# Vector engine waits moved to the next piece of work, and an expert factor read straight from its PSUM bank

## The chip, the cores and the metric

The kernel runs on one core of one Trainium2 chip. Its time is the time of the program on the device in microseconds. Everything else is a row of one profiled execution: TensorE (PE) multiplies matrices into eight banks of 128x512 float32, VectorE (DVE) does elementwise work and reductions, ScalarE (ACT) evaluates activations and copies out of banks, GpSimd (POOL) and SyncE (SP) issue transfers. Engines run their own queues in order and meet at semaphores.

## What is computed

Eight images of 32x32x128 go through six layers, each added to its input. All is float32.

```python
x = x + deformable_conv(_gn(x))        # 9 taps, 4 gathered corners each, weighted, then one matmul
x = x + corr_ranks(_gn(x))             # corr = x3 @ x3.T / c ; sort each row of 1024; take 128 ranks
t = tokens(x)
t = t + window_attention(_ln(t))       # windows of 4, 16, 32
t = t + moe_1(_ln(t))                  # 8 experts, top 2, gelu
t = t + state_space(_ln(t))            # chunked scan
t = t + moe_2(_ln(t))                  # see below

# second layer of the ranks
x_sort = jnp.sort(corr, axis=-1)[..., ::-1]
ranks = jnp.round(jnp.linspace(1.0, m - 1, 128)).astype(jnp.int32)
return x_sort[..., ranks]

# moe_2: the gate is applied to the tokens of the second factor
h1 = jnp.einsum('nc,ehc->neh', flat, w1)
h3 = jnp.einsum('nc,ehc->neh', flat, w3)
h = jax.nn.silu(h1) * h3
y = jnp.einsum('neh,ech->nec', h, w2)
out = jnp.einsum('ne,nec->nc', gates, y)
```

## The kernel before, in words

Four streams of work are woven on every engine. **F** is the first part of an image: group norm, the convolution's indices, 72 gathers of 128 cells (GpSimd), the weighted sums and the convolution, a second group norm, and the correlation of one half. **S** is the sort, on VectorE alone, one unit per half image of 512 tokens: 4 tiles of 128 tokens in two buffers, srt_a and srt_b, 4096 values in a partition. **C** is attention, first experts and state space for a half image. **M** is the second experts for a half image. While image i is sorted, F works on image i+1, C on the second half of i-1 and the first half of i, and M on both halves of i-1. So there are a fill (F alone), an early stage (F, S, C), six full stages (F, S, C, M), a late stage (S, C, M) and a drain (C, M).

Each stream is a generator, and a piece of work ends at a `yield`. The table ORDER holds for each engine and stage a string of letters; `weave` calls the next piece of the stream that the letter names. So the order on each engine is fixed by that table, and an engine whose next piece must wait holds everything behind it.

VectorE must also wait for itself where an instruction reads what the one ahead wrote. `Chain` does this: `link(ins)` lets the instruction count up a semaphore of its stream (dve_F, dve_S, dve_C0, dve_C1, dve_M) and waits for that count at once, at the end of the piece.

The sort (`dve_S`) merges runs of 2, 4, ... 1024. A run of m is merged by a compare of its halves, and then steps of distance m/4, m/8, ... 1. Each step is a max (L813) and a min (L815) of 2048 values at most, from one buffer into the other, and a copy (L817) of the values at both edges of each run that the step leaves alone. Distances m/4 and m/8 are handled apart (L789 to L804). At the end only the 128 ranks are wanted, and three steps (L844) run in the pieces of `rank_pieces`, seven each.

The second experts (`pe_M`, `act_M`, `dve_M`) take three slices (128, 128 and 85 rows) of each of 8 experts per half image, 24 in all. For slice n TensorE multiplies w1 with the tokens into one of two banks (L1517) and w3 with the gated tokens into the other (L1521). ScalarE takes the silu of the first (L1569) into a slot of act2 and copies the second (L1575) into a slot of h3_s; each counts up m_sb, which frees the bank. VectorE multiplies the two slots (L1605, counts up hh), and TensorE uses the product three slices later (L1501). The weights of an expert come in two buffers.

## Time and profile before

| | us |
|---|---|
| runs | 5235.73, 5244.01, 5248.09; median 5244.01 |
| the profiled execution | 5253.13, its span 5251.3 |
| VectorE busy | 4484.3 (85%) |
| TensorE busy | 3963.6 (75%) |
| ScalarE busy | 3017.1 (57%) |
| a full stage, from one image's sort to the next | 601.3 |
| early stage, late stage, drain | 525.5, 567.1, 330.3 |

Busy time is the time that an engine's instructions cover, so where two overlap it is counted once. Stages are cut where the sort of an image starts on VectorE. The mean duration of an instruction is from its start to its end, and can be longer than the distance to the next start.

### The profile page before, as it was taken

Reading aid. Unit: us, or ns where it says so; the run is one execution under the profiler, and the core shown is the slowest. Engines: PE = TensorE matmul, PEld = TensorE weight load, DVE = VectorE, ACT = ScalarE, POOL = GpSimd, SP = SyncE. Lnnn points to the kernel's source line nnn. Section 1 sums busy time; section 2 is a strip of 40 time slices with the busy share of each in tenths; the row PEclk is TensorE's granted clock in tenths of the full one; section 3 lists DMA queues with packets and bytes.
Section 4 is the critical chain, followed back from the end, with each engine's and each line's share of the span. In section 5 each row is a group of like instructions: output and inputs, shape, how many; then the busy total and the mean of one; then the engine's idle time right before and its main releaser. Section 6 shows DMA issues by size and latency. Waiting matters only on the chain.

```text
span 5251.3 us, 59990 instructions
## 1 busy us (share of the span) xinstructions
PE 3963.6 (75%) x19026; PEld 2690.2 (51%) x19026; DVE 4484.3 (85%) x5651; ACT 3017.1 (57%) x7469; POOL 930.2 (18%) x580
## 2 busy tenths in 40 slices
PE   5665628887698877888688877888688877885387
PEld 4544314754366544755357543765357544553254
DVE  0297998899989998899989998999988999999621
ACT  4544326765476635875477645865467646553363
POOL 2253002600054001610045000620036000000000
PEclk8877759999898988988899988988899888886698
DMA  4232001311122011310123001310123001000001
GB/s 131 83 100 65 16 0 55 113 35 30 36 89 83 24 38 39 115 50 23 31 84 101 24 29 42 109 58 23 30 73 109 28 25 30 27 29 14 8 22 36
DMA packets 226079, 269.70 MB, mean 51 GB/s; under 512 B 26831, under 2 KB 188506, under 8 KB 225626
## 3 DMA queue, kind: packets, MB, share of 16 engines
q0 software_dynamic: 46080, 151.03, 9.6%
q1 hardware_dynamic: 179674, 114.65, 7.5%
q8 instruction: 165, 2.70, 0.2%
q14 instruction: 160, 1.31, 0.1%
HBM read 242.25 MB, written 23.34 MB: 51 GB/s over the span
## 4 chain that ended last, share of the span: by engine, by line
DVE 40%; PE 29%; issue 13%; ACT 6%; DMA 5%; SPq 4%; POOL 3%; DVEq 0%; ACTq 0%; POOLq 0%
PE bank L597 6%; DMA gath<-quads,idx 4%; DVE srt_b L772 4%; DVE srt_a L772 4%; PE bank L1204 3%; DVE srt_a L815 3%; POOL gath L735 3%; SPq L502 3%; DVE srt_b L815 3%; DVE srt_a L813 2%; DVE srt_b L804 2%; PE bank L607 2%; DVE srt_a L770 2%; DVE srt_b L813 2%; DVE act L1605 2%
## 5 line engine op out<-in xcount | busy, mean ns | idle before, releaser
L735 POOL DMA_INDIRECT gath<-quads,idx x576 | 930.0, 1615 | 3123.4 <-DVE idx L706 2585.7
L597 PE MATMUL bank<-diag,gath 128*128 128x128 f32 x4608 | 640.6, 303 | 222.3 <-DMA gath<-quads,idx 217.5
L597 PEld LDWEIGHTS bank<-diag,gath 128*128 128x128 f32 x4608 | 615.5, 217 | 269.6 <-DMA gath<-quads,idx 141.9
L630 ACT ACTIVATE diag<-ident,w 128x128 f32<-128x128 f32 x2304 | 696.3, 391 | 12.0 <-DVE w L719 12.0
L1517 PE MATMUL bank<-mu_t,e2w 128*128 128x512 f32 (+1 forms) x768 | 460.5, 685 | 198.6 <-DMA e2w<-moe_w_t 168.0
L1501 PEld LDWEIGHTS bank<-e2w,act 128*128 128x128 f32 (+1 forms) x3072 | 448.1, 214 | 212.3 <-issue 167.4
L1501 PE MATMUL bank<-e2w,act 128*128 128x128 f32 (+1 forms) x3072 | 450.8, 297 | 40.4 <-DVE act L1605 40.4
L1605 DVE TENSOR_TENSOR act<-act,h_s 128x512 f32<-128x512 f32 (+1 forms) x384 | 262.2, 686 | 243.0 <-ACT h_s L1575 231.1
L1521 PE MATMUL bank<-gated_u,e2w 128*128 128x512 f32 (+1 forms) x768 | 456.8, 680 | 15.3 <-ACT h_s L1575 11.7
L1569 ACT ACTIVATE act<-bank 128x512 f32<-128x512 f32 (+1 forms) x384 | 228.2, 594 | 347.8 <-PE bank L1517 345.8
L813 DVE TENSOR_TENSOR srt_a<-srt_b 128x1920 f32<-128x1920 f32 (+5 forms) x176 | 381.5, 2167 | 4.8 <-DVE arena L1421 0.3
L813 DVE TENSOR_TENSOR srt_b<-srt_a 128x1792 f32<-128x1792 f32 (+4 forms) x176 | 378.9, 2153 | 3.7
L815 DVE TENSOR_TENSOR srt_a<-srt_b 128x1920 f32<-128x1920 f32 (+5 forms) x176 | 380.6, 2162 | 0.2 <-DVE carry L1421 0.2
L815 DVE TENSOR_TENSOR srt_b<-srt_a 128x1792 f32<-128x1792 f32 (+4 forms) x176 | 377.9, 2147 | 0.2 <-DVE arena L1421 0.2
L770 DVE TENSOR_TENSOR srt_b<-srt_a 128x2048 f32<-128x2048 f32 x128 | 293.2, 2290 | 5.3 <-DVE srt_a L772 2.5
L772 DVE TENSOR_TENSOR srt_b<-srt_a 128x2048 f32<-128x2048 f32 x128 | 292.5, 2285 | 0.2
L1575 ACT ACTIVATE h_s<-bank 128x512 f32<-128x512 f32 (+1 forms) x384 | 227.3, 592 | 111.5 <-PE bank L1521 109.8
L663 ACT ACTIVATE cols<-bank 128x384 f32<-128x384 f32 x192 | 92.9, 484 | 318.1 <-PE bank L597 306.4
L770 DVE TENSOR_TENSOR srt_a<-srt_b 128x2048 f32<-128x2048 f32 x112 | 256.4, 2289 | 3.4 <-issue 0.5
L772 DVE TENSOR_TENSOR srt_a<-srt_b 128x2048 f32<-128x2048 f32 x112 | 255.5, 2281 | 0.0
L1517 PEld LDWEIGHTS bank<-mu_t,e2w 128*128 128x128 f32 (+1 forms) x768 | 127.6, 201 | 243.9 <-issue 128.9
L1521 PEld LDWEIGHTS bank<-gated_u,e2w 128*128 128x128 f32 (+1 forms) x768 | 144.3, 201 | 208.7 <-issue 150.6
(319 smaller groups left out, 7562.1 us busy)
## 6 DMA issues: line engine op xcount, KB each, us to landing
e2w<-moe_w_t SPq DMA_DIRECT2D x256, 170.5 KB
quads<-xn_tok SPq DMA_DIRECT2D x256, 64.0 KB
e1w<-L_ffn_w SPq DMA_DIRECT2D x256, 64.0 KB, 1.9
e2w<-moe_w_t SPq DMA_DIRECT2D x256, 64.0 KB
gath<-quads,idx POOLq DMA_INDIRECT x576
e2w<-moe_w_t SPq DMA_DIRECT2D x128, 42.5 KB
x_tok<-x SPq DMA_DIRECT2D x8, 512.0 KB, 4.0
out<-tm SPq DMA_DIRECT2D x16, 256.0 KB, 2.5
```

The source lines that it names most:

```text
L597: ins = T.matmul(FB[q % 2][:, k * P:(k + 1) * P], gath[:, g % 2, k, s * C:(s + 1) * C], diag[:, g % 2, 4 * k + s], start=(s == 0), stop=(s ...
L630: ins = SC.activation(diag[:, g % 2, n], ident[:], ACT.Copy, scale=w[:, n:n + 1])
L735: pool.indirect_dma_start(gath[:, g % 2, k], None, quads, bass.IndirectOffsetOnAxis(idx[:, TG * g + k:TG * g + k + 1], 0)).then_inc(sem["g ...
L770: V.tensor_tensor(dst[:, :, 0:size // 2], lo, hi, ALU.max)
L772: link(V.tensor_tensor(dst[:, :, size // 2:size], lo, hi, ALU.min), name)
L813: V.tensor_tensor(y[:, :, :, 0], x[:, :, :, 0], x[:, :, :, 1], ALU.max)
L815: V.tensor_tensor(y[:, :, :, 1], x[:, :, :, 0], x[:, :, :, 1], ALU.min)
L1501: ins = T.matmul(MB[2][:, t * P:(t + 1) * P], act2[0:m, n % ACT2_SLOTS, t * P:(t + 1) * P], e2w[0:m, e % 2, W2 + k * C:W2 + (k + 1) * C], ...
L1517: T.matmul(MB[r % 2][0:m, :], e2w[:, e % 2, k * P:k * P + m], mu_t[:], start=True, stop=True).then_inc(sem["m_ps"], 1)
L1521: T.matmul(MB[r % 2][0:m, :], e2w[:, e % 2, W3 + k * P:W3 + k * P + m], gated_u[:], start=True, stop=True).then_inc(sem["m_ps"], 1)
L1569: SC.activation(act2[0:m, n % ACT2_SLOTS], MB[r % 2][0:m, :], ACT.Silu).then_inc(sem["m_sb"], 1)
L1605: V.tensor_tensor(act2[0:m, n % ACT2_SLOTS], act2[0:m, n % ACT2_SLOTS], h3_s[0:m, n % H3_SLOTS], ALU.mult).then_inc(sem["hh"], 1)
```

## The change

Three things change in the text, and with them the tables of the order.

`Chain` gets `put` (count up) beside `wait`, and in many places the wait stands at the start of the stream's next piece, no longer at the end of this one: all of the sort, the index arithmetic of F, the routing of both experts, parts of the state space, and the layer statistics. Where another engine's semaphore is counted by the same instruction (corr_used, m_ge, g_e, state), VectorE waits on that.

The sort's steps are arranged in twos. A step of distance k writes from one buffer (`here`) into the other, and the step k/2 back from it into `here`, so that only those edge values are copied which the second step reads; runs of 4 are finished in place. The last three steps run in the groups of `rank_groups`: 2, 4 and 7 instructions for 7, 7 and 7.

In the second experts ScalarE's copy and its buffer h3_s go. VectorE's multiply reads the second factor from the bank, and `bank_free` lets TensorE write the bank again after the multiply (hh) where it held the second factor, and after ScalarE (m_sb) where it held another.

```diff
-def rank_pieces():
-    pieces = []
+def rank_groups(k):
+    assert all(r // 8 == c for c, r in enumerate(RANKS))
+    groups = []
     for c, r in enumerate(RANKS):
-        if pieces and r == pieces[-1][2] + 8 * pieces[-1][1]:
-            pieces[-1][1] += 1
+        if groups and groups[-1][2] == r % 8 // k:
+            groups[-1][1] += 1
         else:
-            pieces.append([c, 1, r])
-    return pieces
+            groups.append([c, 1, r % 8 // k])
+    return groups
-            def inc(self, ins):
+            def put(self, ins):
                 ins.then_inc(sem[self.name], 1)
                 self.n += 1
             def wait(self):
                 self.eng.wait_ge(sem[self.name], self.first + self.n)
-            def __call__(self, ins, name=None):
-                self.inc(ins)
+            def __call__(self, ins):
+                self.put(ins)
                 self.wait()
-                if name:
-                    self.eng.sem_inc(sem[name], 1)
...
                 while k >= 1:
-                    x, y = (b[:, :, k:m - k].rearrange("p r (c s k) -> p r c s k", s=2, k=k) for b in (here, there))
-                    V.tensor_tensor(y[:, :, :, 0], x[:, :, :, 0], x[:, :, :, 1], ALU.max)
-                    yield
-                    V.tensor_tensor(y[:, :, :, 1], x[:, :, :, 0], x[:, :, :, 1], ALU.min)
-                    x, y = (b.rearrange("p r (c k) -> p r c k", k=k)[:, :, ::m // k - 1] for b in (here, there))
-                    link(V.tensor_copy(y, x))
-                    yield
-                    now = 1 - now
-                    here, there = there, here
-                    k //= 2
+                    lo, hi = pairs(here, k)
+                    out_lo, out_hi = pairs(there, k)
+                    link.wait()
+                    V.tensor_tensor(out_lo, lo, hi, ALU.max)
+                    yield
+                    if m == 4:
+                        link.put(V.tensor_tensor(hi, lo, hi, ALU.min))
+                        yield
+                        link.wait()
+                        link.put(V.tensor_copy(lo, out_lo))
+                        yield
+                        break
+                    if k == 1:
+                        V.tensor_copy(edges(there, 0, 1), edges(here, 0, 1))
+                    elif k < m // 4:
+                        V.tensor_copy(edges(there, 1, k // 2), edges(here, 1, k // 2))
+                    link.put(V.tensor_tensor(out_hi, lo, hi, ALU.min))
+                    yield
+                    if k == 1:
+                        now = 1 - now
+                        break
+                    link.wait()
+                    if k == m // 4:
+                        for e, a, b in ((1, here, there), (3, there, there), (5, there, here)):
+                            lo, hi = eighth(a, e), eighth(b, e + 1)
+                            ops = [(e, ALU.max), (e + 1, ALU.min)]
+                            for out, side in (reversed(ops) if e == 1 else ops):
+                                ins = V.tensor_tensor(eighth(here, out), lo, hi, side)
+                            if e < 5:
+                                yield
+                        link.put(ins)
+                        yield
+                    else:
+                        lo, hi = pairs(there, k // 2)
+                        out_lo, out_hi = pairs(here, k // 2)
+                        V.tensor_tensor(out_lo, lo, hi, ALU.max)
+                        yield
+                        link.put(V.tensor_tensor(out_hi, lo, hi, ALU.min))
+                        yield
+                    k //= 4
                 m *= 2
...
         def stats(dve, link, src, st, m, name):
             for t in range(UT):
+                if t == UT - 1:
+                    link.put(ins)
                 ins = V.bn_stats(st[:, t], src[:, t])
-            link(ins)
+            link.wait()
             settle(dve)
+            link.put(ins)
             for t in range(UT):
+                if t == UT - 1:
+                    link.wait()
+                    settle(dve)
                 ins = V.bn_aggr(m[:, t], st[:, t:t + 1])
             ins.then_inc(sem[name], 1)
...
             yield
+            def bank_free(n):
+                e, k = divmod(n - 2, 7)
+                if n < 2:
+                    return
+                if k in (2, 4, 6):
+                    pe.wait_ge(sem["hh"], unit("hh", i, h, 3 * e + k // 2))
+                else:
+                    pe.wait_ge(sem["m_sb"], unit("m_sb", i, h, 4 * e + (k + 1) // 2 + 1))
             def gate_u(e):
                 n = 7 * e
                 pe.wait_ge(sem["gate_diag"], unit("gate_diag", i, h, e + 1))
-                if n >= 2:
-                    pe.wait_ge(sem["m_sb"], unit("m_sb", i, h, n - 1))
+                bank_free(n)
                 for t in range(UT):
                     if k == 0:
                         pe.wait_ge(sem["e2_in%d" % (e % 2)], unit("e2_in%d" % (e % 2), i, h, 80 * (e // 2 + 1)))
-                    if r >= 2:
-                        pe.wait_ge(sem["m_sb"], unit("m_sb", i, h, r - 1))
+                    bank_free(r)
                     T.matmul(MB[r % 2][0:m, :], e2w[:, e % 2, k * P:k * P + m], mu_t[:], start=True, stop=True).then_inc(sem["m_ps"], 1)
                     yield
                     r += 1
-                    pe.wait_ge(sem["m_sb"], unit("m_sb", i, h, r - 1))
+                    pe.wait_ge(sem["m_sb"], unit("m_sb", i, h, 4 * e + 1))
+                    bank_free(r)
                     T.matmul(MB[r % 2][0:m, :], e2w[:, e % 2, W3 + k * P:W3 + k * P + m], gated_u[:],
...
                 yield
-                r += 1
-                act.wait_ge(sem["m_ps"], unit("m_ps", i, h, r + 1))
-                if n >= H3_SLOTS:
-                    act.wait_ge(sem["hh"], unit("hh", i, h, n - H3_SLOTS + 1))
-                SC.activation(h3_s[0:m, n % H3_SLOTS], MB[r % 2][0:m, :], ACT.Identity).then_inc(sem["m_sb"], 1)
-                yield
                 if k == 1 and e < E8 - 1:
                     gate_diag_of(e + 1)
...
             for n in range(3 * E8):
                 m = HTILES[n % 3]
-                dve.wait_ge(sem["m_sb"], unit("m_sb", i, h, 7 * (n // 3) + 3 + 2 * (n % 3)))
-                V.tensor_tensor(act2[0:m, n % ACT2_SLOTS], act2[0:m, n % ACT2_SLOTS], h3_s[0:m, n % H3_SLOTS],
+                r = 7 * (n // 3) + 2 + 2 * (n % 3)
+                dve.wait_ge(sem["m_sb"], unit("m_sb", i, h, 4 * (n // 3) + 2 + n % 3))
+                dve.wait_ge(sem["m_ps"], unit("m_ps", i, h, r + 1))
+                V.tensor_tensor(act2[0:m, n % ACT2_SLOTS], act2[0:m, n % ACT2_SLOTS], MB[r % 2][0:m, :],
                                 ALU.mult).then_inc(sem["hh"], 1)
                 yield
             link.end()

```

The tables are new for nearly all engines and stages; one line of VectorE's early stage shows their kind:

```diff
     DVE_early=(
-        "SSSSSSSSFFSFSFSSSSSSSSSSSSSSSSFFFFFSSSSSSSSSSSSSSSSSSSSSSSSSSSSSSSSSSSSSSSSSSSSSSSSSSSSSSSSSSSSS"
+        "SSSSSSSSSFSSFSSSFSSFSSSSSSSSSSSSSSSFSSFSSFFSSFSSSSSSSSSSSSSSSSSSSSSSSSSSSSSSSSSSSSSSSSSSSSSSSSSSS"
```

What that makes of the order is shown at two places. On VectorE in the first full stage, near the end of the merge of 512 values (dve_S is the sort's count of its own; L1605 is the multiply), before:

```order
L813 TENSOR_TENSOR srt_b<-srt_a 128x8x31x8 [waits dve_S]
L1605 TENSOR_TENSOR act<-act,h_s 128x512 [waits m_sb]
L815 TENSOR_TENSOR srt_b<-srt_a 128x8x31x8
L817 COPY srt_b<-srt_a 128x8x2x8
L813 TENSOR_TENSOR srt_a<-srt_b 128x8x63x4 [waits dve_S]
L815 TENSOR_TENSOR srt_a<-srt_b 128x8x63x4
L817 COPY srt_a<-srt_b 128x8x2x4
L1605 TENSOR_TENSOR act<-act,h_s 128x512 [waits m_sb,dve_S]
L813 TENSOR_TENSOR srt_b<-srt_a 128x8x127x2
L815 TENSOR_TENSOR srt_b<-srt_a 128x8x127x2
L817 COPY srt_b<-srt_a 128x8x2x2
L813 TENSOR_TENSOR srt_a<-srt_b 128x8x255 [waits dve_S]
```

and the same steps of the sort after, where L1659 is the multiply, L811 and L847 the max and L827 and L849 the min:

```order
L1659 TENSOR_TENSOR act<-act,bank 85x512 [waits m_ps,m_sb]
L811 TENSOR_TENSOR srt_a<-srt_b 128x8x127x2 [waits dve_S]
L826 COPY srt_a<-srt_b 128x8x2
L827 TENSOR_TENSOR srt_a<-srt_b 128x8x127x2
L847 TENSOR_TENSOR srt_b<-srt_a 128x8x255 [waits dve_S]
L849 TENSOR_TENSOR srt_b<-srt_a 128x8x255
L1659 TENSOR_TENSOR act<-act,bank 128x512 [waits m_ps,m_sb]
L771 TENSOR_TENSOR srt_a<-srt_b 128x4x512 [waits dve_S]
L773 TENSOR_TENSOR srt_a<-srt_b 128x4x512
L1659 TENSOR_TENSOR act<-act,bank 128x512 [waits m_ps,m_sb]
```

Before, a multiply stood between a max and its min, and the sort's wait directly behind the min or its copy. Now max and min stand together and the multiply between one step and the next, ahead of the instruction that carries the wait.

On TensorE in the same stage, second experts between matmuls of the first experts (L1131) and of the group norm, before; L1501 uses the product:

```order
L1131 MATMUL bank<-arena,ident 128x512 [waits gy]
L1517 MATMUL bank<-mu_t,e2w 128x512 [waits m_sb]
L1131 MATMUL bank<-arena,ident 128x512 [waits gy]
L1521 MATMUL bank<-gated_u,e2w 128x512 [waits m_sb]
L1501 MATMUL bank<-e2w,act 128x128 [waits hh]
L1501 MATMUL bank<-e2w,act 128x128 x3
L1517 MATMUL bank<-mu_t,e2w 85x512 [waits m_sb]
L1521 MATMUL bank<-gated_u,e2w 85x512 [waits m_sb]
L1501 MATMUL bank<-e2w,act 128x128 [waits hh]
L1501 MATMUL bank<-e2w,act 128x128 x3
```

and after, where L1574 and L1579 are the products with w1 and w3, L1559 uses the multiply's result and L506 starts the second group norm:

```order
L1574 MATMUL bank<-mu_t,e2w 128x512 [waits m_sb]
L1164 MATMUL bank<-e1w,arena 128x128 [waits gy,gelu]
L1164 MATMUL bank<-e1w,arena 128x128 x3
L1171 MATMUL bank<-arena,ident 128x512 [waits gy]
L1579 MATMUL bank<-gated_u,e2w 128x512 [waits hh,m_sb]
L1559 MATMUL bank<-e2w,act 128x128 [waits hh]
L1559 MATMUL bank<-e2w,act 128x128 x3
L1171 MATMUL bank<-arena,ident 128x512 [waits gy]
L1574 MATMUL bank<-mu_t,e2w 85x512 [waits m_sb]
L506 MATMUL bank<-ident,xn_tok 128x128 [waits x1]
L506 MATMUL bank<-ident,xn_tok 128x128 x3
L1579 MATMUL bank<-gated_u,e2w 85x512 [waits hh,m_sb]
```

Before, the product with w3 waited for ScalarE alone (m_sb). Now it waits for the multiply as well (hh), and between the product with w1 and that with w3 stand pieces of other streams more often.

## Rows read from the trace of the kernel before

**Rows 1.** The page, busy us, share of the span and instructions of each engine:

```profile
span 5251.3 us, 59990 instructions
...
PE 3963.6 (75%) x19026; PEld 2690.2 (51%) x19026; DVE 4484.3 (85%) x5651; ACT 3017.1 (57%) x7469; POOL 930.2 (18%) x580
```

**Rows 2.** Windows: an early, a full, the late stage, the drain; each engine's busy us:

```profile
234.00:759.50 525.50, 273.84 (x1255) 196.60 (x1254) 488.00 (x509) 192.69 (x542) 121.44 (x72) 0.71 0.15 45
...
1956.20:2557.50 601.30, 487.13 (x2378) 331.52 (x2378) 559.11 (x707) 374.26 (x932) 123.53 (x72) 0.89 0.18 55
...
4353.90:4921.00 567.10, 376.15 (x1530) 236.21 (x1530) 549.37 (x662) 276.61 (x595) 0.00 (x0) 0.77 0.07 21
4921.00:5251.30 330.30, 259.86 (x1126) 165.65 (x1126) 78.15 (x211) 185.54 (x391) 0.00 (x0) 0.89 0.09 26
```

**Rows 3.** VectorE's waits in one full stage: us in total, times, longest:

```profile
DVE act L1605 <- ACT h_s L1575: 9.9, 5, 4.9
```

**Rows 4.** VectorE's timeline in the same stage: start us, duration us, instruction:

```profile
2004.93 0.22 DVE L547 SCALAR_TENSOR_TENSOR mv<-mv 128x1 f32<-128x1 f32 x1
2005.07 0.68 DVE L1605 TENSOR_TENSOR act<-act,h_s 128x512 f32<-128x512 f32 x1
2005.67 1.22 DVE L789 TENSOR_TENSOR srt_b<-srt_a 128x1024 f32<-128x1024 f32 x1
2006.81 1.22 DVE L791 TENSOR_TENSOR srt_b<-srt_a 128x1024 f32<-128x1024 f32 x1
2008.06 1.29 DVE L804 TENSOR_TENSOR srt_a<-srt_a,srt_b 128x512 f32<-128x512 f32 x2
```

**Rows 5.** Instructions by shape, VectorE: busy us, mean ns, idle us before:

```profile
L770 DVE TENSOR_TENSOR srt_b<-srt_a 128x2048 f32<-128x2048 f32 x128 | 293.2, 2290 | 5.3 <-DVE srt_a L772 2.5
...
L878 DVE BATCH_NORM_AGGREGATE lnmv<-lnst 128x2 f32<-128x6 f32 x192 | 18.2, 157 | 7.3 <-DVE lnst L874 5.9
```

**Rows 6.** Edge copies in two groups by line, over all shapes; then by shape:

```profile
L817 DVE COPY srt_a<-srt_b 128x256 f32<-128x256 f32 (+5 forms) x176 | 66.2, 376 | 0.0
...
L817 DVE COPY srt_b<-srt_a 128x512 f32<-128x512 f32 (+4 forms) x176 | 56.1, 319 | 0.0
...
L813 DVE TENSOR_TENSOR srt_a<-srt_b 128x1024 f32<-128x1024 f32 x16 | 33.1, 2070 | 0.3
...
L817 DVE COPY srt_b<-srt_a 128x512 f32<-128x512 f32 x64 | 30.3, 473 | 0.0
L844 DVE TENSOR_TENSOR srt_a<-srt_b 128x336 f32<-128x336 f32 x64 | 29.4, 499 | 0.0
...
L817 DVE COPY srt_a<-srt_b 128x256 f32<-128x256 f32 x48 | 15.7, 327 | 0.0
```

**Rows 7.** VectorE by shape: the multiply, one with a bank operand, one without:

```profile
L1605 DVE TENSOR_TENSOR act<-act,h_s 128x512 f32<-128x512 f32 x256 | 175.4, 687 | 195.1 <-ACT h_s L1575 188.8
...
L1037 DVE TENSOR_TENSOR arena<-bank,band 128x960 f32<-128x960 f32 x32 | 36.8, 1151 | 0.8
...
L1411 DVE TENSOR_TENSOR arena<-arena,dtx 128x1024 f32<-128x1024 f32 x16 | 19.6, 1225 | 0.5
```

**Rows 8.** The page, costliest groups: ScalarE's copy of the second factor:

```profile
L1575 ACT ACTIVATE h_s<-bank 128x512 f32<-128x512 f32 (+1 forms) x384 | 227.3, 592 | 111.5 <-PE bank L1521 109.8
```

**Rows 9.** TensorE's waits in the same full stage:

```profile
PE bank L1517 <- DMA e2w<-moe_w_t: 20.9, 7, 3.5
PE bank L597 <- DMA gath<-quads,idx: 18.2, 8, 5.0
```

**Rows 10.** Waits in the early stage:

```profile
DVE bst L537 <- ACT yn_t L521: 27.1, 1, 27.1
```

**Rows 11.** Drain: the last half image's experts as a window:

```profile
5145.60:5247.80 102.20, 80.66 (x339) 50.86 (x338) 16.55 (x24) 39.42 (x81) 0.00 (x0) 0.87 0.11 31
```

**Rows 12.** Drain, timeline from one expert to the next:

```profile
5187.27 0.69 DVE L1605 TENSOR_TENSOR act<-act,h_s 85x512 f32<-85x512 f32 x1 [1.91 <-ACT h_s L1575]
...
5191.72 1.78 PE L1517 MATMUL bank<-mu_t,e2w 128*128 128x512 f32 x2 [3.33 <-DMA e2w<-moe_w_t]
```

207 lines of the change are left out of this document (109 added, 98 removed).

## Prediction

> **What bounds the kernel now.** I read the page's busy line first, then the windows by stage, then VectorE's waits inside one stage, then its timeline. The profiled execution took 5253.13 us, 9 above the median of the runs, 5244.01; its span is 5251.3, and VectorE is the busiest engine with 4484.3 [rows 1]. The windows say where: each of the six full stages of about 600 us (the experts of one image, the sort and the middle layers of the next, the convolution of the one after) has VectorE busy for 559 of 601.3 us, TensorE for 487 and ScalarE for 374; the late stage has it busy for 549 of 567, and only the drain (78 of 330) is not its own [rows 2]. So a microsecond taken from VectorE's queue in a full stage is a microsecond of the stage, as long as the others feed it in time. Of its 42 idle us there, some 27 are waits for others, the largest 9.9, the multiplies of the second experts for ScalarE's copy [rows 3]; the other 15 are in pieces of 35 to 150 ns.
>
> Those pieces are its own waits. In the timeline an instruction that waits for nothing of its own starts before the end of the one ahead (2005.67 against 2005.07 + 0.68, 2006.81 against 2005.67 + 1.22), and one that waits for the one ahead starts 0.03 after its end (2008.06 against 2006.81 + 1.22) [rows 4]. The size of the overlap: L878's 192 instructions of 157 ns sum to 30.1 us but cover 18.2, and 144 of them follow one another, so 83 ns each; behind a wait L770 stands idle 5.3 us in 128, 41 ns with a few longer ones, usually 35 [rows 5]. **Price of a wait for the instruction directly ahead: 35 + 83 = 118 ns.**
>
> **Part 1, the moved waits.** In the program's order I counted, per full stage, the instructions that wait for a count of VectorE's own. Before there are 270, all directly behind their producer. After there are 278, of which 168 stand behind their own stream; at the other 110 a piece of another stream stands in between, the shortest of them longer than 83 ns. 102 stalls fewer at 118 ns are 12.0 us per stage. In the fill and early part 49 fewer (5.8 us), in the late stage about 87 (10.3).
>
> Here the Trainium skill speaks against the change: its page "VectorE: DVE Perf Modes", section "The DRAIN you can't avoid", has eight copies with a semaphore after each and with one at the end take the same time, so that the semaphore "costs nothing extra here". By that rule this part is worth 0 and the stage gains 5.8 us instead of 17.8. The trace disagrees: the overlap of 83 ns is there without a wait and gone with one. I follow the trace and keep the rule as a rival.
>
> **Part 2, the sort's instructions.** Max and min halves are the same. Per half image, 22 edge copies (122.3 us in 352, so 7.64 per half) become 13. From the rows by size: one of 1024 single elements has no row; copies of 512 cost 0.42 to 0.63 (30.3 us in 64, those with single elements dearer) and a max of 1024 elements at this stride 2.07, twice its usual price. So it lies between 0.68 and 2.07, and I take 1.10, the rate of the dearer 512. One of 512: 0.63. Five of 256 at 0.31: 1.56. Six of 16 to 128, at 0.18 to 0.27, a little over the fixed part of an instruction (below): 1.24. Sum 4.53, so 3.1 less, of which 9 x 0.083 was overlapped anyway: 2.35 per half [rows 6]. The last three steps go from 21 instructions to 13 with the same elements; 336 elements cost 499 ns and 2048 cost 2290, that is 1.04 ns for an element and 0.15 us fixed; less the 0.083 overlapped, 8 x 0.07 = 0.55 [rows 5, 6]. Together 2.9 per half, 5.8 per stage (3.8 to 6.6 with the ends of the unknown copy).
>
> **Part 3, the second factor from the bank.** VectorE's multiply stays 48 per stage. From the bank it costs the same: 960 elements with a bank operand take 1151 ns and 1024 from SBUF 1225, which at the 1.04 ns just found leaves 150 and 160 fixed; the multiply's own 687 leaves 155 [rows 7]. The Trainium skill's same page, in the table of its section on the TRN2 errata, gives a bank source 62 cycles more than an SBUF source; that would be 65 ns each, 3 us per stage. The rows show nothing of it. ScalarE loses 48 copies of 592 ns, 28 us per stage, but it isn't the bound [rows 8]. What it costs is slack. Before, the bank was free once ScalarE had copied it, and VectorE could lag by three slots. Now TensorE's next product with the gated tokens (L1579) waits for the multiply, and the multiply for that product: queued behind L1579 on TensorE stand gather products and middle-layer matmuls, on which VectorE's other pieces depend. 48 such handovers per stage. The cover is VectorE's own order: summed from the rows, nearly every pair of multiplies has 4.8 us or more of sort between them, and one product is 0.69 long. Two arrivals can break it: expert weights (20.9 us of TensorE's waits in a stage) and gathers (18.2) [rows 9]. Against that, the new order puts the second norm of the convolution's image some 90 us of VectorE time later (391 instead of 300 into the stage), so that gathers have far more room. Bounds: the 9.9 us wait goes wholly (-10), or each of the 48 handovers loses as long a wait as one multiply, 0.69 (+33). Nearest to the rows of full stages, where five waits make up the 9.9, I take +2 per stage, 12 in all.
>
> **Early, late, drain.** In the early stage 5.8 + 5.8 = 11.6 less. But the gather indices stand about 16 us of VectorE's time later in it, and the norm that waits for the convolution only 13 later; its wait of 27.1 us grows to about 30 [rows 10]. So -8.6. Late: 10.3 + 5.8 = -16. Drain: experts there are paced by TensorE and the weights' transfer. A new expert starts 3.33 us late for it at half speed, 102.2 us for one half image's experts with VectorE busy 16.6; the multiply waits 1.91 for the copy, but TensorE needs it three steps later [rows 11, 12]. That wait shrinks and nothing ends sooner: -1.
>
> **Sum.** Six full stages 6 x 17.8 = 106.8, less 12, plus 8.6, 16 and 1: 120 us less. 5253 - 120 = 5133 in the profile's own terms; against the runs' median 5244 - 120 = 5124. What is late next: real waits of 27 to 30 us per stage, and TensorE, 487 busy of then 585.
>
> **Rivals.**
> A. The handover costs a good part: 5 to 15 us per stage rather than 2. For it: two rigid orders now meet 48 times a stage with a single bank as buffer. Against: gathers are spread. Gain 120 - 6 x 8 = 72, down to 25: 5172 to 5219.
> B. Slower: the handover becomes the pace of the experts. One mechanism: L1579 stands behind a late gather or late weights, the next multiply waits at the head of VectorE's queue and holds the sort with it. If it happens at each of the 16 experts of a stage with the mean of today's five waits, 2.0 us, that is 32 us per stage instead of 2: 5124 + 180 = 5304. It decides from about 20 us more per stage, ten such stalls. Against it: today there are five.
> C. Waits save nothing: the instruction behind a satisfied wait starts no earlier than one behind its own producer, because the pipe must empty in any case. Then only part 2 is left: 8 x 5.8, about 46, less 12: 5210. Against it speaks the start of L1605 at 2005.07, behind a wait long satisfied, 0.08 before the end of the instruction ahead (2004.93 + 0.22) [rows 4]. The Trainium skill's section named above is what would have it so.
> D. More than the sum: with indices early enough, gathers spread and ScalarE relieved, the real waits shrink too, by 5 to 10 us per stage: 5064 to 5094.
>
> **Chances.** Forecast (5095 to 5172) 0.54; A 0.12; B 0.07; C 0.06; D 0.16; no change, by a mixture of A and C, 0.05. The range for 8 in 10 takes the forecast, D and most of A: 5060 to 5195. What this measurement can tell from no change is 0.2%, 10 us: faster 0.88 (forecast, A, C, D), same 0.05, slower 0.07.
>
> **What would show it.** In the profile after: full stages of 580 to 588 us; VectorE's busy time per stage down by some 14 to 545 (5.8 of instructions, and 102 overlaps of 83 ns, which it counts once); the idle pieces of 35 ns fewer by a third, 3.6 us; edge copies about 72 us in all, with the one of 1024 near 1.1; the multiply still at 0.69. The waits of the multiply on TensorE would be the coupling: up to 12 us per stage confirms the sum, 20 or more is A or B. If stages stay near 600 with as many 35 ns pieces gone, part 1 was wrong in price. If the early stage isn't shorter, the gather's later start ate it.

## The result: 271 us less, more than twice the forecast

| | us | ratio to before, 95% interval |
|---|---|---|
| before, 4 runs beside it | 5246.05 | |
| after, 4 runs (4970.38 to 4978.58) | 4974.92 | 0.9485 [0.9467, 0.9502] |
| predicted | 5124, range 5060 to 5195 | |

The gain is 271 us where 120 were forecast, and the time lies outside the range. The profiled execution took 4978.58. Its page and its windows, which answer to [rows 1, 2] (early, full, late stage, drain; each engine's busy us with its instructions, then granted clock, DMA share, GB/s):

```profile
span 4976.7 us, 59038 instructions
...
PE 3775.6 (76%) x19026; PEld 2594.7 (52%) x19026; DVE 4375.1 (88%) x5379; ACT 2911.1 (58%) x7170; POOL 966.8 (19%) x580
```

```profile
231.60:736.60 505.00, 268.47 (x1255) 193.49 (x1254) 477.74 (x476) 192.63 (x542) 117.15 (x72) 0.72 0.16 47
1862.60:2425.70 563.10, 454.39 (x2378) 313.56 (x2378) 545.39 (x671) 363.85 (x898) 131.02 (x72) 0.90 0.20 59
4112.70:4657.00 544.30, 368.32 (x1530) 231.85 (x1530) 533.65 (x624) 258.66 (x552) 0.00 (x0) 0.81 0.07 21
4657.00:4976.70 319.70, 258.38 (x1126) 163.38 (x1126) 77.88 (x213) 159.60 (x344) 0.00 (x0) 0.89 0.09 27
```

A full stage is 563.1 us instead of 601.3, 38 less where 16 (17.8 less 2) were forecast. The early stage lost 20.5 (forecast 8.6), the late one 23 (16), the drain 11 (1), the fill 2. The six full stages together lost 218 of the 275 by which the two spans differ, so the full stage is where to look.

VectorE's part of it, from the gaps in the two traces, for the stage of [rows 2]:

| one full stage, us | before | after | difference |
|---|---|---|---|
| VectorE busy | 559.1 | 545.4 | -13.7 |
| idle pieces of 30 to 49 ns | 7.6 (219) | 5.3 (152) | -2.4 |
| idle pieces of 50 to 299 ns | 7.3 (51) | 1.6 (7) | -5.7 |
| waits of 300 ns or more | 27.3 | 10.8 (9) | -16.5 |

The first two rows are near the forecast (545, and a third fewer pieces, though these give 2.4 us and not 3.6). The third had no term of its own in the prediction, and the fourth had been expected to grow by 2. What is left of VectorE's waits for others, to be read against the 9.9 us of [rows 3]:

```profile
DVE act L1659 <- PE bank L1579: 2.6, 2, 1.7
DVE mst L905 <- issue: 2.3, 1, 2.3
DVE act L1659 <- ACT act L1627: 2.0, 3, 1.3
DVE dtx L1422 <- ACT dtr L1350: 1.7, 1, 1.7
DVE arena L1485 <- PE bank L1307: 1.6, 2, 1.0
```

None is over 2.3 us long. Before, two others of the first four were the layer statistics of the state space and the token update, which have shrunk to 0.3 or gone:

```profile
DVE lnst L874 <- ACT td L1165: 8.4, 1, 8.4
DVE tm L1450 <- PE bank L1279: 3.5, 1, 3.5
```

Both end behind TensorE, the second directly and the first through ScalarE's L1165, which had itself waited for the first experts' last product on TensorE (L1131). TensorE's waits for transfers before were those of [rows 9] and one more; after, in the same stage, the only one for a transfer left is the first of these two, and the second is the new coupling of the bank:

```profile
PE bank L1112 <- DMA e1w<-L_ffn_w: 7.4, 1, 7.4
```

```profile
PE bank L593 <- DMA gath<-quads,idx: 8.7, 5, 3.1
PE bank L1579 <- DVE act L1659: 7.5, 5, 3.8
```

So 46.5 us of TensorE's waiting for weights and gathers became 8.7. The prediction had cited these waits only as something that could break the handover, not as something that an order could remove. What TensorE has to spare now lies mainly in one piece at the seam of two stages, where it has run ahead and waits for a layer norm of ScalarE:

```profile
PE bank L925 <- ACT mu L919: 57.2, 1, 57.2
```

TensorE's busy time in the stage fell too, from 487.1 to 454.4 us, with the same 2378 instructions. The granted clock accounts for it. Of the busy time, 109.9 us before and 45.8 us after lie in stretches at the lower of its two levels (1.2 instead of 2.4 GHz); counted at half, they leave 432.2 and 431.5 us of work at full speed. Before, such a stretch follows the waits for weights, as in this one (two timeline rows with start and duration, and a window with a granted clock of 0.50):

```profile
2455.49 2.07 PE L1517 MATMUL bank<-mu_t,e2w 128*128 128x512 f32 x2 [3.44 <-DMA e2w<-moe_w_t]
2463.69 1.02 PE L1517 MATMUL bank<-mu_t,e2w 128*85 128x512 f32 x2
```

```profile
2454.60:2461.40 6.80, 5.91 (x13) 3.54 (x14) 6.73 (x6) 1.20 (x2) 0.00 (x0) 0.50 0.01 4
```

After, the longest stretch at the lower level lies mostly in the wait of 57.2 us, where TensorE has nothing to do. So the mean clock of a stage, 0.89 and 0.90, hides what changed.

The instructions, answering to [rows 5 to 7], VectorE by shape (busy us, mean ns, idle before):

```profile
L1659 DVE TENSOR_TENSOR act<-act,bank 128x512 f32<-128x512 f32 x256 | 174.5, 682 | 144.7 <-PE bank L1579 124.4 <-ACT act L1627 19.9
...
L815 DVE TENSOR_TENSOR srt_b<-srt_b 128x1024 f32<-128x1024 f32 x16 | 33.4, 2085 | 0.0
...
L818 DVE COPY srt_b<-srt_a 128x1024 f32<-128x1024 f32 x16 | 18.2, 1135 | 0.3
```

The multiply takes 682 ns from the bank, 687 from SBUF before: no extra, as forecast. The Trainium skill's page "VectorE: DVE Perf Modes", in its table on the TRN2 errata, adds 62 cycles for a bank source; this trace doesn't show them. The unknown copy of 1024 single elements costs 1.135 us (1.10 was chosen), and all edge copies together 73.6 (72).

### The profile page after: what moved, and what is told of

Read it like the earlier page. It is cut to its first block, busy times and chain, and to the rows that moved or that the text cites. A ratio compares the mean times of both kernels' runs of the same rounds, so it can differ in the third digit from the quotient of the medians.

```text
span 4976.7 us, 59038 instructions
## 1 busy us (share of the span) xinstructions
PE 3775.6 (76%) x19026; PEld 2594.7 (52%) x19026; DVE 4375.1 (88%) x5379; ACT 2911.1 (58%) x7170; POOL 966.8 (19%) x580
## 4 chain that ended last, share of the span: by engine, by line
DVE 40%; PE 35%; issue 14%; ACT 4%; DMA 3%; POOL 2%; SPq 1%; DVEq 0%; ACTq 0%; POOLq 0%
PE bank L593 6%; DVE srt_a L773 4%; PE bank L1579 4%; PE bank L1574 4%; DVE srt_b L773 4%; PE bank L1559 4%; DVE srt_a L827 3%; DVE srt_a L811 3%; PE bank L1244 3%; DMA gath<-quads,idx 2%; POOL gath L736 2%; DVE srt_a L839 2%; DVE srt_b L771 2%; DVE srt_a L771 2%; DVE srt_b L849 2%
## 5 line engine op out<-in xcount | busy, mean ns | idle before, releaser
L736 POOL DMA_INDIRECT gath<-quads,idx x576 | 966.6, 1678 | 2933.9 <-DVE idx L705 2028.9
L593 PE MATMUL bank<-diag,gath 128*128 128x128 f32 x4608 | 605.8, 293 | 157.8 <-DMA gath<-quads,idx 156.9
L593 PEld LDWEIGHTS bank<-diag,gath 128*128 128x128 f32 x4608 | 585.5, 208 | 194.3 <-DMA gath<-quads,idx 126.0
L1559 PEld LDWEIGHTS bank<-e2w,act 128*128 128x128 f32 (+1 forms) x3072 | 420.1, 202 | 163.6 <-issue 159.8
L1579 PE MATMUL bank<-gated_u,e2w 128*128 128x512 f32 (+1 forms) x768 | 435.2, 650 | 75.1 <-DVE act L1659 72.4
L1574 PE MATMUL bank<-mu_t,e2w 128*128 128x512 f32 (+1 forms) x768 | 441.0, 658 | 55.0 <-DMA e2w<-moe_w_t 36.6
L1559 PE MATMUL bank<-e2w,act 128*128 128x128 f32 (+1 forms) x3072 | 426.7, 286 | 1.2 <-DVE act L1659 1.2
L1659 DVE TENSOR_TENSOR act<-act,bank 128x512 f32<-128x512 f32 (+1 forms) x384 | 261.2, 680 | 181.6 <-PE bank L1579 155.1
L811 DVE TENSOR_TENSOR srt_a<-srt_b 128x1024 f32<-128x1024 f32 (+3 forms) x208 | 384.2, 1847 | 1.1
L827 DVE TENSOR_TENSOR srt_a<-srt_b 128x1024 f32<-128x1024 f32 x192 | 351.3, 1830 | 0.0
L1579 PEld LDWEIGHTS bank<-gated_u,e2w 128*128 128x128 f32 (+1 forms) x768 | 132.5, 191 | 238.3 <-issue 161.1
L847 DVE TENSOR_TENSOR srt_b<-srt_a 128x2016 f32<-128x2016 f32 (+1 forms) x96 | 211.8, 2206 | 0.8
```

The source lines that it names most:

```text
L593: ins = T.matmul(FB[q % 2][:, k * P:(k + 1) * P], gath[:, g % 2, k, s * C:(s + 1) * C], diag[:, g % 2, 4 * k + s], start=(s == 0), stop=(s ...
L736: pool.indirect_dma_start(gath[:, g % 2, k], None, quads, bass.IndirectOffsetOnAxis(idx[:, TG * g + k:TG * g + k + 1], 0)).then_inc(sem["g ...
L811: V.tensor_tensor(out_lo, lo, hi, ALU.max)
L827: link.put(V.tensor_tensor(out_hi, lo, hi, ALU.min))
L1559: ins = T.matmul(MB[2][:, t * P:(t + 1) * P], act2[0:m, n % ACT2_SLOTS, t * P:(t + 1) * P], e2w[0:m, e % 2, W2 + k * C:W2 + (k + 1) * C], ...
L1574: T.matmul(MB[r % 2][0:m, :], e2w[:, e % 2, k * P:k * P + m], mu_t[:], start=True, stop=True).then_inc(sem["m_ps"], 1)
```

## The experiments

Three things can be undone apart: the waits with the sort's instructions (W), the order of the tables (O), and the reading of the second factor from the bank (B). Twelve kernels were run, each beside runs of before on the same chip (medians 5246 to 5257). The eight ways to combine the three stand in the table under 8, where before counts as 5250, its median beside runs 1 to 4.

**1. The waits back where they were.** Under the new order every `put` waits at once.

```diff
-            def put(self, ins):
+            def inc(self, ins):
                 ins.then_inc(sem[self.name], 1)
                 self.n += 1
-            def wait(self):
+            def put(self, ins):
+                self.inc(ins)
                 self.eng.wait_ge(sem[self.name], self.first + self.n)
+            def wait(self):
+                pass
```

Expected: 

> The kernel after, with its order of pieces, but each chain wait of VectorE stands at once behind its instruction again (the few waits on corr_used, g_e, m_ge and state stay moved). Per full stage 262 instructions instead of 168 wait directly behind their producer. If a moved wait is worth what the two profiles show for 102 of them (16.6 us per stage, 0.163 us each), 94 come back as 15 us per stage and 20 to 25 outside the full stages: about 5090 us (5075 to 5110), with full stages of 575 to 580. At the 118 ns of the prediction: 5057. If the semaphore costs nothing extra, as the rival from the Trainium skill has it, 4975.

Measured: 5078.82, ratio 0.9673 [0.9656, 0.9690], 104 us over after. Its full stage, and the same place of the routing in after and in this kernel (start us, duration us):

```profile
1894.70:2471.50 576.80, 457.57 (x2378) 314.37 (x2378) 553.45 (x672) 364.19 (x899) 130.01 (x72) 0.89 0.20 57
```

```profile
2210.80 0.19 DVE L1109 TENSOR_TENSOR gv<-gv,gsm 128x32 f32<-128x32 f32 x1
2210.99 0.69 DVE L1659 TENSOR_TENSOR act<-act,bank 128x512 f32<-128x512 f32 x1
2211.59 0.18 DVE L1112 TENSOR_TENSOR gv<-gv,rev 128x32 f32<-128x32 f32 x1
```

```profile
2252.90 0.19 DVE L1109 TENSOR_TENSOR gv<-gv,gsm 128x32 f32<-128x32 f32 x1
2253.31 0.69 DVE L1659 TENSOR_TENSOR act<-act,bank 128x512 f32<-128x512 f32 x1 [0.21 <-DVE gv L1109]
```

Waits directly behind their producer are 262 in its full stage against 168, and the stage is 13.7 us longer: 0.146 each. VectorE's busy time is 8.1 more and its idle pieces under 300 ns 9.7 more, together 17.8 or 0.19 for each wait; 4.1 of that came back, since its waits for others fell from 10.8 to 6.7. In the two timelines the multiply starts 0.19 after L1109 began where it stands between put and wait, and 0.41 where the wait stands directly behind L1109. So the lost overlap is what was forecast, and where the next piece begins with a wait of its own, the idle time here is 0.2 us and not 0.035. Theory C falls, and with it, for this kernel, what the Trainium skill has in "VectorE: DVE Perf Modes", section "The DRAIN you can't avoid", that a semaphore after each instruction "costs nothing extra here": by that this run would have taken 4975.

**2. The sort's instructions back** (all edges copied at every step, the last three steps in seven instructions each), new order, moved waits:

```diff
-                    if k == 1:
-                        V.tensor_copy(edges(there, 0, 1), edges(here, 0, 1))
-                    elif k < m // 4:
-                        V.tensor_copy(edges(there, 1, k // 2), edges(here, 1, k // 2))
+                    if k < m // 4:
+                        V.tensor_copy(sides(there, k), sides(here, k))
...
                         link.put(V.tensor_tensor(out_hi, lo, hi, ALU.min))
+                        V.tensor_copy(sides(here, k // 2), sides(there, k // 2))
```

Expected: 

> The kernel after, with its order and moved waits, but the sort's edge copies in full (22 per half image) and the last three steps in seven instructions each. By the rows of before this is 2.9 us per half image: 16 x 2.9 = 46, so 5021 us (5010 to 5030). If the gain beyond the sum came from the sort, for instance because shorter pieces let others in earlier, it is over 5060.

Measured: 5010.43, ratio 0.9539 [0.9520, 0.9558], 35 over after. The full stage has VectorE busy for 551.3 against 545.4, 5.9 more where 5.8 were forecast, but is only 3.3 longer: its waits for others fell from 10.8 to 9.0. Instructions were priced right, and a part of them came back as a shorter wait.

**3. The kernel after under the tables of before.** Only the strings change (TensorE, ScalarE and VectorE run their pieces in before's order; an empty piece stands for ScalarE's copy):

```diff
     ACT_full=(
-        "FMCMMFCCFFCFMCCCFFFFFFCCCFCFCMCFFMMCMCMMCCMFMMMMFCCMCCCFCCCCCCCCCCCFCMCFMCMMCCFFCMFFCFFFCCFCCCCC"
+        "FMCCCMFCFMCCCFFFFFCCFMFCCMCCFMMCMMCFMCMFCFFMMCCFCCCCCCCCCCCCCCCFCFMCMCCCFCFFCCFFCCFMMCCCFFFCFFCC"
...
```

Expected: 

> The code after (moved waits, new sort, factor read from the bank) under the tables of before; the sort's min and copy for runs of four are one piece again, and ScalarE has an empty piece where its copy was. In this order only 36 instead of 102 stalls go per full stage (234 of 278 directly behind). Theory 1, that the surplus of about 16 us per stage comes from the new order: a stage is 601 - 5.8 (sort) - 36 x 0.16 (waits) = 589 to 590, in all about 5155 us (5130 to 5200). Theory 2, that it comes from the bank read (no ScalarE copy to wait for, ScalarE relieved): another 16 us per stage less, about 5060 (5040 to 5085). A third: in an order not made for it the handover between TensorE and VectorE costs, and it is over 5246.

Measured: 5316.77, ratio 1.0130 [1.0112, 1.0147]: 1.3% slower than before and 342 over after, which is what the third theory had. Its full stage, VectorE's waits in it and TensorE's:

```profile
1958.20:2572.00 613.80, 486.15 (x2378) 329.04 (x2378) 551.45 (x671) 349.09 (x884) 127.50 (x72) 0.89 0.19 54
```

```profile
DVE arena L1485 <- PE bank L1307: 14.6, 5, 9.0
DVE act L1660 <- PE bank L1579: 12.9, 4, 6.8
DVE lnst L905 <- ACT td L1205: 9.0, 1, 9.0
```

```profile
PE bank L595 <- DMA gath<-quads,idx: 27.6, 9, 8.9
PE bank L1574 <- DMA e2w<-moe_w_t: 20.8, 7, 3.5
PE bank L1579 <- DVE act L1660: 19.2, 9, 4.2
```

VectorE is busy only 6 us more than after the whole change, and the stage is 51 us longer. Here the handover is what rival B described: TensorE waits 19.2 us for multiplies, 7.5 after. And the waits for weights and gathers are back. The old tables also leave fewer pieces to stand between a put and its wait: 234 waits are directly behind their producer, where the new tables have 168 and before has 270. This is the run that showed the failed step: **the order isn't neutral**.

**4. The kernel before with the bank read alone** (old waits, old sort, old order):

```diff
-                SC.activation(h3_s[0:m, n % H3_SLOTS], MB[r % 2][0:m, :], ACT.Identity).then_inc(sem["m_sb"], 1)
...
+                dve.wait_ge(sem["m_ps"], unit("m_ps", i, h, r + 1))
-                V.tensor_tensor(act2[0:m, n % ACT2_SLOTS], act2[0:m, n % ACT2_SLOTS], h3_s[0:m, n % H3_SLOTS],
+                V.tensor_tensor(act2[0:m, n % ACT2_SLOTS], act2[0:m, n % ACT2_SLOTS], MB[r % 2][0:m, :],
```

Expected: 

> The kernel before with one edit: VectorE reads the second factor from the bank, the bank is freed by the multiply, ScalarE's copy is gone (an empty piece in its place). Theory 2 (the bank read brings the surplus): the waits of 9.5 and 8.5 us per full stage go, 5246 - 6 x 16 = about 5150 us. Theory 1 (the order brings it): within 20 us of 5246. If the handover costs without its own order: 5270 or more, with VectorE waiting for TensorE's product ahead of the multiply.

Measured: 5355.13, ratio 1.0204 [1.0180, 1.0228], 105 more than before. In its full stage TensorE waits for multiplies 11 times:

```profile
PE bank L1529 <- DVE act L1610: 18.9, 11, 4.3
```

and VectorE stands 38.5 us in waits for others instead of 27.3. By itself the simplification is a loss of 2%.

**5. ScalarE's copy put back under the new order.** The copies are pieces of a stream of their own, H, which ScalarE begins at the first place where their product was there in the trace of after:

```diff
+        def act_H(act, i, h):
+            for n in range(3 * E8):
+                m = HTILES[n % 3]
+                r = 7 * (n // 3) + 2 + 2 * (n % 3)
+                act.wait_ge(sem["m_ps"], unit("m_ps", i, h, r + 1))
+                if n >= H3_SLOTS:
+                    act.wait_ge(sem["hh"], unit("hh", i, h, n - H3_SLOTS + 1))
+                SC.activation(h3_s[0:m, n % H3_SLOTS], MB[r % 2][0:m, :], ACT.Identity).then_inc(sem["hc"], 1)
+                yield
...
-                    pe.wait_ge(sem["hh"], unit("hh", i, h, 3 * e + k // 2))
+                    pe.wait_ge(sem["hc"], unit("hc", i, h, 3 * e + k // 2))
```

Expected: 

> The kernel after with ScalarE's copy of the second factor put back: the bank is freed by the copy, VectorE multiplies from the buffer of three slots. All other pieces stand as after; each copy stands in ScalarE's order at the first piece that starts after its product is done in the profile of after. If the surplus over the sum comes from the order and the bank read only shifts work, this is within 30 us of 4975 (28 us of copies per stage go beside ScalarE's 364 of 563). If the bank read itself brings it, by shortening the way from product to multiply or by relieving ScalarE, 50 to 150 us are lost: 5025 to 5125. If the handover without slack costs in the new order too, this is faster than after, 4950 or less.

Measured: 5095.09, ratio 0.9694 [0.9676, 0.9712], 120 over after. VectorE's waits in a full stage:

```profile
DVE act L1671 <- ACT act L1630: 10.1, 7, 3.7
DVE act L1671 <- ACT h_s L1649: 3.7, 5, 1.3
DVE dtx L1455 <- ACT ecum L1370: 2.9, 2, 2.7
```

TensorE no longer waits for a multiply at all, yet VectorE waits 26.2 us instead of 10.8. It isn't the copy that is late (3.7), but what ScalarE does beside it, the silu of the other factor (10.1) and the decay (2.9).

**6. The new order alone:** run 5 with the old waits and the old sort as well.

Expected: 

> All three edits undone under the new order: waits at once, full edge copies and seven-instruction ranks, ScalarE's copy; only the order of the pieces is that of after (with the copies' places of e5). If parts add up: 4975 + 104 (e1) + 35 (e2) + the difference of e5. With e5 near after about 5115 us, so that the order alone is worth about 130 of the 271 us. If the order is only good with what it was made for, it is 5200 or more.

Measured: 5202.84, ratio 0.9897 [0.9875, 0.9918], 47 less than before. The expected 5115 held for a run 5 near after. With the 120 us that run 5 cost, the recorded sum is 4975 + 104 + 35 + 120 = 5234, so undoing all three costs 31 us less than one by one. VectorE's waits for others shrink from 27.3 to 15.4 a stage against before.

**7. Waits and sort alone:** before's order and copy, the other two edits.

Expected: 

> The other corner: the order of before with ScalarE's copy kept, but moved waits and the new sort. Against before 36 stalls fewer per full stage at 0.15 us and the sort's 35 us (e2): 5250 - 35 - 40 = about 5175 us. Against e3 (bank read in the same order, 5317) it shows what the handover without slack costs there: about 140 us; e4 against before gave 105. If it is near 5317, the cost of e3 was not the bank read but the waits or the sort in a foreign order.

Measured: 5243.92 in ten runs, ratio 0.9979 [0.9961, 0.9998], 6 to 8 less. VectorE is busy for 551.1 of a stage of 603.8, 8 less than before, its small idle pieces are down too, and its waits for others are up from 27.3 to 44.2:

```profile
DVE arena L1486 <- PE bank L1308: 14.4, 4, 10.4
DVE act L1660 <- ACT h_s L1630: 10.5, 6, 4.6
DVE lnst L906 <- ACT td L1206: 9.8, 1, 9.8
```

What VectorE saves it waits away. TensorE is then the engine that others are late behind: its waits for transfers have grown from 46.5 to 54.3 us, 25.1 for gathers instead of 18.2, and 20.9 and 8.3 for weights, nearly as before.

**8. New order and bank, with old waits and old sort** (edits 1 and 2 together).

Expected: 

> The new order and the bank read, with the waits at once and the sort's old instructions. Additive under this order: 4975 + 104 + 35 = 5114, full stages near 581. Rival: where both are taken away, some of VectorE's time is lost in waits for others anyway, so less than the sum: 5080 to 5095. Rival: the order holds only as long as VectorE keeps up, so more than the sum, 5150 or above, with real waits over 20 us in a full stage.

Measured: 5116.16, ratio 0.9745 [0.9716, 0.9774], 141 over after. The two are additive here (104 + 35 = 139), with 4.9 us of waits for others in a stage, the fewest of all. This completes the table, times in us:

| | W old | W new | W is worth |
|---|---|---|---|
| order old, copy | 5250 (before) | 5244 | -6 |
| order old, bank | 5355 | 5317 | -38 |
| order new, copy | 5203 | 5095 | -108 |
| order new, bank | 5116 | 4975 (after) | -141 |

The column W must be read with care, because W is not the same change in every row. Under the old tables it takes 36 waits a stage from behind their producer, under the new ones 94 and more. VectorE's own time in a stage (busy, and idle pieces under 300 ns) falls by 14.5 us from before to run 7 and by 22.7 from run 8 to after; its waits for others grow by 16.9 and 5.9. So of the 19 us a stage between -6 and -141, about 8 were never saved under the old order, and 11 were saved and waited away.

No edit has a price of its own. The bank read costs 105 or 73 under the old order and saves 87 or 120 under the new one. The order is worth 47 with nothing else and 342 with both others.

**9. ScalarE's time without its dependence.** At the place of each copy of run 5 ScalarE copies as many elements of a constant, and nothing waits for it; the rest is the kernel after.

```diff
-                SC.activation(h3_s[0:m, n % H3_SLOTS], MB[r % 2][0:m, :], ACT.Identity).then_inc(sem["hc"], 1)
+                SC.activation(h3_s[0:m, n % H3_SLOTS].rearrange("p (a b) -> p a b", a=UT),
+                              ident[0:m].unsqueeze(1).to_broadcast([m, UT, P]), ACT.Identity)
```

Expected: 

> The kernel after, with ScalarE doing at the place of each of the 48 copies of a stage a copy of the same size that nothing waits for and that waits for nothing. Theory 'ScalarE's time': its other pieces, the silu of the next slice above all, come 0.6 us later each time and VectorE waits for them: 5060 to 5100, the multiply's wait for the silu near the 9.8 us of a stage that the true copy had. Theory 'the longer way': nothing depends on the copy, so 4975 to 5000.

**10. The dependence with a third of the time:** ScalarE copies one column of each second factor, the multiply waits for that and reads the bank.

```diff
-                SC.activation(h3_s[0:m, n % H3_SLOTS], MB[r % 2][0:m, :], ACT.Identity).then_inc(sem["hc"], 1)
+                SC.activation(h3_s[0:m, n % H3_SLOTS, 0:1], MB[r % 2][0:m, 0:1], ACT.Identity).then_inc(sem["hc"], 1)
```

Expected: 

> The kernel after, with a ScalarE copy of one column (some 0.2 us in place of 0.6) of each second factor: ScalarE waits for TensorE's product there, and the multiply waits for ScalarE, but reads the bank, which it frees as in the kernel after. Theory 'the longer way', in which ScalarE's queue stands behind a product that is late: 5060 to 5110. Theory 'ScalarE's time': a third of it remains, 4985 to 5020.

Measured: 5037.38 for run 9, ratio 0.9594 [0.9564, 0.9624], 62 over after, and 5063.67 for run 10, 0.9651 [0.9622, 0.9680], 89 over. Neither theory holds alone. The multiply's wait for the silu, first in run 9 and then in run 10:

```profile
DVE act L1669 <- ACT act L1630: 6.5, 4, 2.8
```

```profile
DVE act L1672 <- ACT act L1630: 7.6, 7, 3.3
```

Both make ScalarE's next piece late, one by working and one by standing in its queue behind a product of TensorE (22.8 us a stage ahead of the copies of one column). Run 5, with both, costs 120, less than 62 + 89; it isn't their plain sum, since there the copy also frees the bank.

**11 and 12. Fewer waits still.** The kernel after keeps 168 waits directly behind their producer in a full stage, 135 of them in pieces of the other streams. Such pieces are cut at the wait, and an instruction of another stream stands in the cut: in run 11 only where no other engine waits for the piece, or where its input had long been there so that it could begin earlier; in run 12 everywhere.

```diff
-            link(V.scalar_tensor_tensor(gv[:], oh[:], NEG, gl[:], ALU.mult, ALU.add))
+            link.put(V.scalar_tensor_tensor(gv[:], oh[:], NEG, gl[:], ALU.mult, ALU.add))
+            yield "cut"
+            link.wait()
```

Expected of 11: 

> The kernel after, with VectorE's pieces of the other streams cut at their inner waits and a max, a min or a multiply put into the cut, only where no other engine waits for the piece or where its input had been there long enough to begin it earlier. Waits directly behind their own producer fall from 168 to 124 in a full stage, 131 to 99 in the early and 156 to 115 in the late one. At 0.146 us each: 6.4 a stage, 6 x 6.4 + 4.7 + 6.0 = 49 less, 4926. At the prediction's 0.118: 40 less, 4935. Rival: the time saved is lost in waits for others, as it was under the old order (waits and sort together only 6): 4965 to 4980.

Expected of 12: 

> The same with all such pieces cut, so that results which other engines wait for come one or two sort steps (1.2 to 4.6 us) later, some 60 times in a full stage: 73 waits directly behind their producer are left of 168. If the chains of the other engines have slack: 95 x 0.146 = 13.9 a stage, about 102 less in all, 4873. If order and lateness decide, as in the runs with the copy put back: real waits of VectorE grow by more than 14 us a stage and the time is 4980 or above.

Measured: 5009.09 for run 11, ratio 0.9536 [0.9505, 0.9566], 34 over after (27 by the two ratios, since before was 10 slower beside this run); 5183.94 for run 12, 0.9865 [0.9830, 0.9900], 209 over. Their full stages:

```profile
1870.90:2438.20 567.30, 455.66 (x2378) 315.41 (x2378) 542.31 (x672) 363.95 (x898) 124.87 (x72) 0.90 0.20 58
```

```profile
1932.30:2522.80 590.50, 460.74 (x2378) 319.76 (x2378) 539.68 (x672) 363.36 (x898) 137.10 (x72) 0.89 0.19 56
```

In run 11 the 44 removed waits give nearly what they should: VectorE's busy time falls by 3.1 us and its idle pieces under 300 ns by 2.5, 0.127 for each. But its waits for others go from 10.8 to 20.6, and the stage is 4.2 longer. In run 12 they go to 46.9. Its largest:

```profile
DVE act L1742 <- PE bank L1660: 9.1, 6, 4.3
DVE act L1742 <- ACT act L1708: 8.0, 6, 3.9
DVE lnst L926 <- ACT tbu L1088: 5.6, 1, 5.6
```

A shift of one or two instructions of VectorE, with the other engines' orders left as they are, costs more than 44 or 95 waits bring. No version here beats the kernel after.

## Why the prediction was wrong

**What bounds the kernel** was right: VectorE is busy for 545.4 of 563.1 us, and TensorE still isn't the bound (454).

**Part 1, the moved waits.** Forecast 12.0 per full stage for 102 of them, 88 in all; run 1, which puts 94 back, measured 13.7 and 104. The mechanism was right and its price too low, 118 ns where VectorE lost 189 and the stage 146. The overlap in it was right (8.1 us of busy time for 94); the idle time was not, because 35 ns is what a wait leaves whose follower has nothing else to wait for. The table's row of 50 to 299 ns (51 pieces before, 7 after) is of other kinds: at 29 of the 51 the next instruction waits for one more semaphore, and at most of the others VectorE counts one up by itself between the wait and the next instruction, which makes it 0.15 us. The pieces "of 35 to 150 ns" stood in the first paragraph of the prediction and got one price.

**Part 2, the sort's instructions.** Forecast 5.8 per stage, 46 in all; run 2 measured 5.9 us of busy time, but a stage only 3.3 longer and 35 in the end, since VectorE's waits and its other idle pieces got shorter.

**Part 3, the bank.** The price of the multiply was right (0.68). The handover was forecast to cost 2 us a stage, 12 in all, with ScalarE's 28 us of copies worth nothing since "it isn't the bound". Measured under the new order, the bank read saves 87 without W and 120 with it. An engine with 35% of its time free still delays others when it must run one more piece ahead of the one that is waited for; runs 9 and 10 show this from both sides. The danger that was described is real, but belongs to the old order (runs 3 and 4: 19 us of TensorE's waiting for multiplies a stage, and a slower kernel).

**The failed step** is the term "+2 per stage, 12 in all", the whole of what the prediction gave to waits for others. Measured, they fell by 16.5, which lies outside even the bounds that the prediction gave this term (-10 to +33), because the lower one let only the multiply's wait go. Over the six full stages these waits fell by 90 us where 12 more were forecast, 102 of the 151 us by which the forecast was off. The prediction priced the edits one by one and let the tables only carry them. But TensorE's waits for transfers, 46.5 us in a stage of before, are 8.7 in after, and in the other kernels with the new tables they are as short (7.7 in run 8, 4.7 in run 5, 4.9 in run 6). Its busy time at the lower clock goes the same way: 103 to 119 us a stage in the four kernels with the old tables, 46 to 66 in the ten with the new ones or tables made from them, whatever else they do. That is TensorE's room of some 70 us a stage. With it 141 us of W reach the end, where 6 did under the old order, part of that because W moves fewer waits there. The new place of the second norm, 90 us later, stood in the prediction as room for gathers, and it drew no number from it. That experts stand further apart on TensorE it did not read from the order at all: before, the last seven of a stage's 16 start 13.8 to 15.2 us after one another, most of them after a wait of over 3 us for weights; after, no two are closer than 17.3 us, and no wait for their weights is left.

**The rivals.** A's times don't follow from its own condition: 5 to 15 us a stage instead of 2 leave a gain of 102 to 42, that is 5142 to 5202, and 5172 to 5219 belong to 10 to 18. A and B fall, with 7.5 us of TensorE's waiting for the multiply a stage. C falls with run 1. D was right in its direction and its reasons (gathers spread, ScalarE relieved), but priced at 5 to 10 us a stage where 16.5 came. Its times, 5064 to 5094, still carry the 2 us a stage that it replaces; without them they are 5052 to 5082, and don't reach 4975 either. The early stage's gain of 20.5 against 8.6 has the same error: the norm's wait was to grow from 27.1 to about 30 and fell to

```profile
DVE bst L533 <- ACT yn_t L517: 21.7, 1, 21.7
```

What stays open: which of the tables' moves makes the room, and how much of it is worth what. The order was exchanged as a whole; moving the experts alone, or the norm and the gathers alone, wasn't tried, and neither was a kernel that changes the clock without the waits. That it is TensorE's room which lets W through is read from the waits of these kernels; no run makes that room by itself. For the same reason the table's cells with the new order and the copy stand for one placement of the copies, chosen from a trace, and a better one may exist.

## What to carry to other kernels

Where fixed orders of several engines meet, price the order as an edit of its own: list who waits for which transfer or engine before, look in the new order whether the distance to it has grown, and give those waits a term of their own, with the work at the lower clock that follows them. Time taken from the busiest engine arrives at the end only if the others are early enough, so what frees it and what lets the others run ahead must be weighed, and tested, together: here the waits and the sort alone gave 6 us, the order alone 47, the bank read alone cost 105, and all three gave 271. Once such an order fits, moving pieces by one place can save VectorE 6 us a stage and still make the stage 4 us longer.

## What the runs showed of the hardware

- A wait of VectorE for its own last instruction costs 0.03 to 0.04 us of idle time and the lost overlap of 0.08; with another stream's wait behind it the start comes 0.41 after the start of an instruction of 0.19, against 0.19 with the wait moved (run 1). Over a stage that is 0.19 of VectorE's time for each, of which 0.146 lengthened the stage.
- A min of 1024 elements, each operand one value in every four, took 2.085 us (L815), and one of 1024 in longer rows 1.22; a copy of as many single values 1.135:

```profile
L827 DVE TENSOR_TENSOR srt_b<-srt_a 128x1024 f32<-128x1024 f32 x48 | 58.5, 1218 | 0.0
```

- TensorE's 96 products with w1 in a full stage took 687 ns in the mean before and 638 after. Before, 16 of them began in stretches at the lower granted clock and took 1055 ns, the other 80 took 614; after, it was 6 at 1084 and 90 at 608. So nearly all that differs is the clock, though its mean over the stage is 0.89 and 0.90. Run 6, under the new tables, has 460.5 us of TensorE at a mean clock of 0.885; before has 487.1 at 0.886: it matters whether the lower clock falls where TensorE works.
